# Fourteen picked groups instead of eleven, the first at group 3; the input check in pieces; the last edge tile as its own group

## The reference

```python
h = relu(layernorm(x))
x = x + sage3(h)          # three SAGE layers: mean over incoming edges @ Wl.T + b + h @ Wr.T, relu between
h = relu(layernorm(x))
messages = gelu((h[src] + edge_attr) @ We1 + be1) @ We2 + be2
aggregated = segment_sum(messages, dst)
x = x + gelu(((1 + eps) * h + aggregated) @ Wu1 + bu1) @ Wu2 + bu2
```

## Time and profile before

| | us |
|---|---|
| median of 3 executions | 976.62 |
| lowest, highest | 975.94, 2135.52 |
| profiled execution | 981.04 |
| its span in the trace | 979.3 |
| PE busy in it | 879.7 (90%) |
| PE weight loads | 653.8 (67%) |
| DVE busy | 485.6 (50%) |
| POOL busy | 383.6 (39%) |
| ACT busy | 250.2 (26%) |

### The profile page before, as it was taken

How to read it: one execution, slowest core, us unless ns; L and a number is a source line. 1 busy time by engine, 2 the same in 40 slices (tenths; PEclk the granted TensorE clock), 3 DMA queues, 4 the chain that set the end, 5 groups by cost and what they waited for, 6 DMA issues and landing times.

```text
span 979.3 us, 20510 instructions
## 1 busy us (share of the span) xinstructions
PE 879.7 (90%) x7824; PEld 653.8 (67%) x7824; DVE 485.6 (50%) x1882; ACT 250.2 (26%) x433; POOL 383.6 (39%) x411
## 2 busy tenths in 40 slices
PE   2977999999999999999809999999999899899883
PEld 1733555555554455555609999998988888898882
DVE  6589999995111121121348545445445545445431
ACT  2576677773110110011102111111111111111111
POOL 2000000000000001111277777777777777777771
PEclk9969999999999999999959999999999999999987
DMA  4200001102000000000174444444434444434321
GB/s 137 63 2 12 3 13 13 12 13 65 1 1 1 1 1 11 11 10 17 49 170 108 134 120 137 133 113 130 138 102 134 117 117 130 117 107 130 106 63 32
DMA packets 46635, 67.90 MB, mean 69 GB/s; under 512 B 15396, under 2 KB 25349, under 8 KB 46402
## 3 DMA queue, kind: packets, MB, share of 16 engines
q1 hardware_dynamic: 34626, 42.11, 15.5%
q0 software_dynamic: 11904, 24.40, 9.8%
HBM read 63.18 MB, written 3.30 MB: 68 GB/s over the span
## 4 chain that ended last, share of the span: by engine, by line
PE 64%; DVE 12%; POOL 10%; issue 7%; DMA 3%; ACT 2%; SPq 0%; ACTq 0%; POOLq 0%; DVEq 0%
PE f_ps L1132 26%; PE f_ps L1183 11%; POOL f_adj L545 10%; PE f_ps L1237 8%; PE f_ps L1168 7%; DVE f_region L594 2%; PE f_ps L1017 2%; DVE f_region L592 2%; PE f_ps L1010 2%; PE f_ps L1107 2%; DVE f_region L598 2%; DVE f_region L596 2%; DMA f_adj<-in_dst_next 1%; DMA inv<-f_rstd 1%; PE f_ps L1069 1%
## 5 line engine op out<-in xcount | busy, mean ns | idle before, releaser
L545 POOL DMA_INDIRECT f_adj<-table,f_table_idx x372 | 359.4, 966 | 113.4 <-issue 112.8
L1132 PE MATMUL f_ps<-f_adj,f_parts 125*128 125x500 fp8e4 (+1 forms) x1575 | 331.5, 352 | 0.1
L1132 PEld LDWEIGHTS f_ps<-f_adj,f_parts 125*128 125x128 bf16 x1575 | 143.5, 97 | 130.0 <-issue 11.1
L1183 PE MATMUL f_ps<-f_parts 125*128 125x128 bf16 x3300 | 200.0, 220 | 0.0
L1183 PEld LDWEIGHTS f_ps<-f_parts 125*128 125x128 bf16 x3300 | 193.2, 98 | 6.4 <-issue 4.4
L530 POOL TENSOR_TENSOR f_rest<-f_region,f_parts 125x512 f32<-125x512 f32 (+1 forms) x7 | 7.3, 1050 | 461.5 <-ACT f_parts L975 461.5
L1237 PE MATMUL f_ps<-f_adj 128*128 128x94 f32 (+20 forms) x984 | 131.9, 280 | 30.3 <-ACT f_adj L997 28.2
L870 DVE TENSOR_TENSOR f_adj<-f_ps,f_adj 128x512 f32<-128x512 f32 x93 | 64.1, 689 | 186.1 <-issue 116.0
L1237 PEld LDWEIGHTS f_ps<-f_adj 128*128 128x128 f32 x984 | 120.9, 195 | 37.9 <-issue 34.3
L997 ACT ACTIVATE f_adj<-f_adj 128x512 f32<-128x512 f32 x93 | 58.4, 630 | 336.8 <-DVE f_adj L870 332.5
L887 ACT CAST f_adj<-f_ps 128x500 f32 x213 | 126.1, 592 | 56.7 <-PE f_ps L1017 40.8
(11 more groups left out here) (135 smaller groups left out, 478.7 us busy)
## 6 DMA issues: line engine op xcount, KB each, us to landing
f_region<-in_edge_attr_T SPq DMA_DIRECT2D x104, 256.0 KB
f_adj<-table,f_table_idx POOLq DMA_INDIRECT x372
f_parts<-in_src_row SPq DMA_DIRECT2D x11, 256.0 KB, 3.7
f_adj<-inv SPq DMA_DIRECT2D x1, 1562.5 KB, 7.7
table<-f_region SPq DMA_DIRECT2D x6, 250.0 KB
out<-f_xT SPq DMA_DIRECT2D x6, 250.0 KB, 2.5
f_rcntT<-inv SPq DMA_DIRECT2D x5, 250.0 KB, 3.8
f_xT<-in_xT SPq DMA_DIRECT2D x1, 812.5 KB, 6.0
```

The costliest lines, as they stand in the source:

```text
L545: pool.indirect_dma_start(out=rows[:, r % RW, j * D:(j + 1) * D], out_offset=None, in_=table, in_offset=bass.IndirectOffsetOnAxis(ap=table ...
L1132: ins = pe.matmul(ps[:, dense_ps(i):dense_ps(i) + width(c)], parts[0:NP, (l % 2) * 3 + p, b, :], adj[0:NP, b, lo:hi].bitcast(F8), start=b ...
L1183: ins = pe.matmul(z_ps(g, j), select[0:NP, u % SELECT, j * P:(j + 1) * P], parts[0:NP, 3 + p, b, :], start=b == 0 and j == 0 and p == 0, s ...
```

## The change

It picks 14 groups instead of 11: 3, 10, 17, 24, 31, 39, 46, 53, 60, 68, 75, 82, 89, 97, so that the first has its 25 blocks in slots 0 to 2 (8, 8 and 9) and the others in the five to seven slots between two picked groups, three to five in each. Groups 0 to 102 have four tiles as before, group 103 has three, and tile 415 is group 104 (`FG` = 105); `tile(g)` gives a group's first tile, and the windows and bounds of the check follow. The check is split: `check_repeats` (the maximum over `c25`) goes into slot `CALM` = 221 of the dense stage, behind the slot's other DVE work; the rest goes into slots 0, 1, 2, 4, 8, 9 and 10 of the edge stage, behind the selections; PE's matmul of the flag moves from slot 0 to slot 12, and `keep_flag` from slot 2 to 13. The padding of the last tile's source numbers is 0, 1, 2, ... instead of zeros.

```diff
-        self.FG = -(-self.FT // self.FTG)
+        self.FG = -(-(self.FT - 1) // self.FTG) + 1
...
-        self.PERIOD = 9
-        self.picked = list(range(self.PERIOD - 1, self.FG - self.FTG, self.PERIOD))
+        self.SHARES = 14
+        reach = self.FG - 2 * self.FTG
+        self.picked = [self.FTG - 1 + i * (reach - self.FTG + 1) // (self.SHARES - 1) for i in range(self.SHARES)]
...
+    def tile(self, g):
+        return min(g * self.FTG, self.FT - 1) if g < self.FG else self.FT
+
     def tiles(self, g):
-        return min(self.FTG, self.FT - g * self.FTG)
+        return self.tile(g + 1) - self.tile(g)
...
+    CALM = GB + 8
...
+    FLAG, KEEP = 12, 13
...
+            def check_repeats():
+                dve.memset(flag[:, :], 0.0).then_inc(cleared, 1)
+                dve.wait_ge(cleared, 1)
+                dve.wait_ge(count_in[0], 16 * ((NC + 1) // 2))
+                dve.wait_ge(count_in[1], 16 * (NC // 2))
+                dve.tensor_reduce(flag[0:NB, 2:3], c25[0:NB, :], AX.X, ALU.max).then_inc(repeats, 1)
+                dve.wait_ge(repeats, 1)
+                dve.tensor_scalar(flag[0:NB, 2:3], flag[0:NB, 2:3], 15.5, None, ALU.is_gt).then_inc(repeats, 1)
...
                 for c in plan.due("rows_add", slot):
                     keep_rows(c)
+                if slot == CALM:
+                    check_repeats()
...
-            check_input()
             for g in range(END):
-                if g == 2:
+                if g == KEEP:
                     keep_flag()
...
                     for i, b in s.selections(g + 1):
                         select_sources(i, b)
-            dve.wait_ge(flagged, 11)
+                if g == 0:
+                    check_tiles()
+                if g == 1:
+                    check_steps()
+                if g == 2:
+                    check_windows()
+                if g == 4:
+                    join_checks()
+                if g == 8:
+                    check_order()
+                if g == 9:
+                    join_order()
+                if g == 10:
+                    join_all()
+            dve.wait_ge(flagged, 8)
...
-                    pe.wait_ge(flagged, 11)
+                    pe.wait_ge(flagged, 8)
...
-                if g == 0:
-                    pe.wait_ge(flagged, 9)
+                if g == FLAG:
+                    pe.wait_ge(flagged, 6)
                     pe.matmul(ps[0:1, 7 * BANK:7 * BANK + 1], flag[:, 3:4], unit[:, 0:1],
                               start=True, stop=True).then_inc(flagged, 1)
...
-    a["src_tiles"] = np.pad(src, (0, pad)).reshape(-1, P).T
+    a["src_tiles"] = np.concatenate([src, np.arange(pad, dtype=src.dtype)]).reshape(-1, P).T
```

More of the change, by code:

```diff
@@ L403, in edge_columns @@
         def edge_columns(g):
-            return t["edge_attr_T"][:, g * T * P:(g * T + s.tiles(g)) * P]
+            return t["edge_attr_T"][:, s.tile(g) * P:s.tile(g + 1) * P]
         def agg_ps(c, lo, hi):
@@ L751, in window_onehots @@
                     ins = dve.tensor_scalar(onehot[:, g % OH, j, 0:hi - lo], iota[:, 0:hi - lo], float(lo),
-                                            dst_abs[:, g * T + j:g * T + j + 1], ALU.add, ALU.is_equal)
+                                            dst_abs[:, s.tile(g) + j:s.tile(g) + j + 1], ALU.add, ALU.is_equal)
                 ins.then_inc(oh_ready, 1)
@@ L788, in node_add, with more, over, check_tiles @@
                                          op0=ALU.add, op1=ALU.add).then_inc(node_added, 1)
-            def check_input():
-                F, L = first[0:1, :], last[0:1, :]
-                F2, L2, FB, LB = F[:, 0:NT:2], L[:, 0:NT:2], F[:, 1:NT:2], L[:, 1:NT:2]
-                DG = s.DG
-                n_at = [0]
-                def more(count):
-                    n_at[0] += count
-                    return viol[0:1, n_at[0] - count:n_at[0]]
-                def over(a, gap, b):
-                    dve.scalar_tensor_tensor(out=more(a.shape[-1]), in0=a, scalar=float(gap), in1=b, op0=ALU.subtract,
-                                             op1=ALU.is_gt).then_inc(checked, 1)
+            F, L = first[0:1, :], last[0:1, :]
+            F2, L2, FB, LB = F[:, 0:NT:2], L[:, 0:NT:2], F[:, 1:NT:2], L[:, 1:NT:2]
+            DG = s.DG
+            n_at = [0]
+            def more(count):
+                n_at[0] += count
+                return viol[0:1, n_at[0] - count:n_at[0]]
+            def over(a, gap, b):
+                dve.scalar_tensor_tensor(out=more(a.shape[-1]), in0=a, scalar=float(gap), in1=b, op0=ALU.subtract,
+                                         op1=ALU.is_gt).then_inc(checked, 1)
+            small = [(0, 0.0, ALU.is_gt), (NT - 1, float(N - s.DW), ALU.is_lt)]
+            small += [(s.DT * (g + 1), float(e), ALU.is_lt) for e, g in zip(s.node_end, s.build_group) if g + 1 < GB]
+            def check_tiles():
                 over(L2, s.A_COLS // NB - 1, F2)
@@ L815, in check_input, with join_checks, check_order @@
                 dve.wait_ge(tile_in, 32)
-                over(bound[0:1, 0, :], 0.0, group_ends[0:1, 0, :])
+                over(bound[0:1, 0, :], s.MARGIN, group_ends[0:1, 0, :])
                 over(group_ends[0:1, 1, :], 0.0, bound[0:1, 1, :])
-                small = [(0, 0.0, ALU.is_gt), (NT - 1, float(N - s.DW), ALU.is_lt)]
-                small += [(s.DT * (g + 1), float(e), ALU.is_lt) for e, g in zip(s.node_end, s.build_group) if g + 1 < GB]
                 for i, limit, op in small:
                     dve.tensor_scalar(more(1), F[:, i:i + 1], limit, None, op).then_inc(checked, 1)
+            def join_checks():
                 dve.wait_ge(checked, 8 + len(small))
-                dve.memset(flag[:, :], 0.0).then_inc(flagged, 1)
-                dve.wait_ge(flagged, 3)
+                dve.wait_ge(cleared, 1)
                 dve.tensor_reduce(flag[0:1, 0:1], viol[0:1, 0:n_at[0]], AX.X, ALU.max).then_inc(flagged, 1)
+            def check_order():
                 dve.wait_ge(order_in, 32)
@@ L866, in _ @@
                         dve.wait_ge(z_ready, g + 1)
-                        dve.wait_ge(gathered[r % RW], 16 * (T * (r // RW) + s.tiles(g)))
+                        dve.wait_ge(gathered[r % RW], 16 * sum(s.tiles(s.of_ordinal(q)) for q in range(r % RW, r + 1, RW)))
                         if r >= PR:
@@ L1799, in layouts @@
     a["edge_attr_T"] = np.pad(ea.T, ((0, 0), (0, pad)))
-    a["src_tiles"] = np.pad(src, (0, pad)).reshape(-1, P).T
+    a["src_tiles"] = np.concatenate([src, np.arange(pad, dtype=src.dtype)]).reshape(-1, P).T
     a["src_row"] = np.pad(src, (0, pad))
     a["dst_tiles"] = np.pad(dst, (0, pad), constant_values=-1).reshape(-1, P).T
-    group = 4 * P
-    a["group_ends"] = np.concatenate([dst[0::group], dst[group - 1::group], dst[-1:]])[None]
+    starts = np.append(np.arange(0, dst.size - P, 4 * P), dst.size // P * P)
+    a["group_ends"] = dst[np.concatenate([starts, starts[1:] - 1, [dst.size - 1]])][None]
     for n in SAGE:
```

26 lines of the change are left out of this document (15 added, 11 removed).

## The result

The changed kernel takes 974.5 us in the median (971.59 to 976.08, 11 executions), the kernel before beside it 977.18: ratio 0.9964 [0.9952, 0.9977]. By the ratio 3.5 us are gained, by the two medians 2.7, where 8.6 were forecast. The profiled executions give 981.04 before and 975.46 after, -5.6. The bound moved as forecast, from POOL to PE, but POOL stands close behind it.

A forecast was written before the change was run, and what follows sets the result against it. POOL's 372 gathers bound the kernel; PE was to become the bound: 495.9 plus 459.7 gives 955.6, plus 3 handovers and 3.6 tail 962.2 against 971.2, so -9.0 us and a median of 968; 80% range 958 to 979.

The forecast's parts named there:

- the start of the selections: PE's first selection in the edge stage: 23.3 us won without the flag wait, 3.0 lost earlier, so 495.9.
- the stall of check_repeats: Dense stage, slot 221: the reduction delays agg(6), so PE stalls 3.0 us before mix(6); bounds 0 and 3.7.
- the sum of PE's steps: PE's edge-stage mixes, sums, selections, nodes and low clock: 459.7 us from 495.9, so the last sum ends at 955.6.
- PE-bound end: Main case: PE's stream sets the edge stage's end; 968 us, range 963 to 974, chance 0.66.
- handover idle: Rival: PE's 28.2 us of waits for messages in the edge stage stay; 993 us (976 to 1000), chance 0.13.
- low clock: Edge stage front: 1.5 us in PE's sum; as a rival about 19 us more over three slots, 985, chance 0.04.
- the added matmuls cost more than the old ones: Rival: the 900 added selection matmuls take 96 ns each instead of 56, 36 us more, 1004; chance 0.02.
- the handovers: Edge stage: PE's waits for gathered rows and other handovers add 3 us, bounds 0 and 10.
- the tail behind the last sum: End of the edge stage, last sum to end of node_add: 3.6 us instead of 4.7, with node_down(5) ahead.
- The median of the runs shown is 976.62, 4.4 below the profiled one, so 967.6: Last step: from the forecast profiled total of 972.0 to the median, said as 968.
- POOL needs 24 x 1.27: Edge stage gathers: 1.27 us per tile, 30.5 us per seven slots, against 32.0 for PE.
- POOL stays the bound: Rival: PE has more room and 360 gathers set the end, the last at 948.1; 961 us (957 to 963), chance 0.15.

The follow-up runs named there:

- e21: Changed kernel with check_repeats in slot 225 and 60 more matmuls in PE's wait before the first selection, on a chip without stalls: 968.05 us, 0.9907 of the kernel before.
- e9: The changed kernel again, unedited, on a chip with stalls: 1215.32 us, 1.0166 of the kernel before.
- e20: The changed kernel again, unedited, on a chip without stalls: 973.9 us, 0.9966 of the kernel before.
- e15: Kernel before with nearly all of PE's edge-stage matmuls left out, on a chip without stalls: 976.04 us, 0.9975 of the whole kernel before.
- e16: Changed kernel with nearly all of PE's edge-stage matmuls left out, on a chip without stalls: 968.91 us, 0.9905 of the whole kernel before.
- e18: e16 with a four-column memset in place of each DVE selection from the thirteenth on: 959.66 us, 0.9821 of the whole kernel before.
- e1: Changed kernel with check_repeats in slot 225 instead of 221, on a chip with stalls: 1205.69 us, 1.0094 of the kernel before.
- e10: e1's edit of the changed kernel again, on another chip with stalls: 1217.08 us, 1.0107 of the kernel before.
- e2: Changed kernel with the eleven picked groups of before, all else as changed, on a chip with stalls: 1218.38 us, 1.013 of the kernel before.
- e4: The kernel before, unedited, on another chip with stalls: 1203.59 us beside 1204.63.
- e12: Changed kernel with 11 of the 12 selection matmuls of each block left out, on a chip with stalls: 1087.21 us beside 1188.43 of the kernel before.
- e14: Kernel before with 11 of the 12 selection matmuls of each block left out, on a chip with stalls: 1090.63 us beside 1188.43 of the whole kernel.
- e3: Changed kernel with the rest of the check ahead of the slot loop and the flag in slot 0, chip with stalls: 1214.12 us, 1.0188 of the kernel before.

## Why the prediction was right or wrong

**Right.** PE as the new bound, the end of its wait for the flag, the start of the selections (495.9 forecast, 496.24 measured), the stall of check_repeats (3.0 forecast, 2.89 and a start of the edge stage 2.96 later), and the sum of PE's steps: 459.7 us forecast, 462.1 busy measured between 496.24 and the end of the last sum at 961.85. The windows all but without a gap and POOL's wait for the add of 0.6 us came as listed. The time, 974.5, lies in the 80% range of 958 to 979, and just outside the 963 to 974 given for a PE-bound end. The two slower rivals did not show: handover idle is 3.5 us, not 28, and eight blocks at the front cost 2.7 us of low clock, not 19. Nor did the added matmuls cost more than the old ones: eight blocks, 96 matmuls, take 5.52 us in e21, 57.5 ns each. (By the 81 ns of the Trainium skill's "TensorE: Matmul & The Clock Gate", "Back-to-back issue gap", they would be an estimated 7.8; the measurement decides.)

**Wrong: the gain.** 8.6 us were forecast, 2.7 (medians) or 3.5 (ratio) measured. Two steps failed, by about 3.5 us each.

The first is a row of small terms of PE's side. The selections start 0.3 later; PE's work is 2.4 more than summed, half of it the low clock at the front (8.06 us for eight blocks instead of 5.36, so 2.7 instead of 1.5), the other half not assigned; the handovers cost 3.5 instead of 3; the tail behind the last sum is 4.1 us instead of 3.6. Together 3.7: the chain ended 5.2 us earlier instead of 9.0. The low clock was mis-sized because it lasted longer than in the earlier trace rows, where it was 0.52 for the first 3 us of work and 1.00 from then on: here it was 0.50 from 496 to 500, 0.80 from 500 to 504 and 1.00 only behind that. The tail had it too (0.55 from 962 to 966); in e9, at 0.93, the tail took 3.2.

The second is the step "The median of the runs shown is 976.62, 4.4 below the profiled one, so 967.6". It took the distance of one execution from its median as a constant. For the changed kernel it was 1.0. Part of that distance is where PE's matmuls change from one rate to the other in the first 40 us. Timelines of PE of the changed kernel, first the profile after, then e20:

```profile
24.16 1.87 PE L1070 MATMUL f_ps<-f_xT,f_cent 128*128 128x500 f32 x2
25.83 1.68 PE L1073 MATMUL f_ps<-f_mean,f_xT 128*125 128x1 f32 x8
...
30.18 1.12 PE L1073 MATMUL f_ps<-f_mean,f_xT 128*125 128x1 f32 x8
```

```profile
23.86 1.00 PE L1070 MATMUL f_ps<-f_xT,f_cent 128*128 128x500 f32 x2
24.71 0.93 PE L1073 MATMUL f_ps<-f_mean,f_xT 128*125 128x1 f32 x8
```

The edge stage starts at 487.77 in the one and 484.37 in the other, and their times are 975.46 and 971.95: nearly all of the 3.5 us between two executions of one kernel is made there. The profiled execution of before changed late as well (L1028, the same matmuls, takes 1.87 us at 24.38 and 28.73), so the two profiles compare fairly, at -5.6.

But its 981.04 lies above every other execution of that kernel on such chips (975.94 to 980.48, the one very long aside). e15, whose dense stage is the same, shows why: it changed early, its edge stage starts at 481.75 instead of 484.81, and its gathers were a chain of 471.5 us instead of 472.5. So 3.1 of the profile's distance from its median come from the first 40 us and 1.0 from gathers. The eleven times of the changed kernel fall into two sets, 971.59 to 972.98 (five) and 974.50 to 976.08 (six); the late profile, 975.46, belongs to the second, and e20's early one, 971.95, would fit the first. So its median lies among the late ones, while that of before seems to lie among the early ones. That is read from the times, and not shown for executions without a profile.

So 3.4 us of the forecast gain (4.4 - 1.0) were a difference between one execution and its median.

**Wrong without effect.** "POOL needs 24 x 1.27", and with it 948.1 for the last gather's end: it was 955.62. A gather took 1.29 us from start to start, not 1.27. The forecast asked of the 19.8 us of selections only whether DVE had room, and not what they do to gathers. e15, e16 and e18 have 1.267, 1.275 and 1.256: selections cost gathers time, but in the kernels with little PE work the added ones, with the check's pieces, make only 0.008 of the 0.02; the rest shows up only with all of PE's work, and its cause stays open. (The Trainium skill's "GPSIMD Engine Reference", "8. Key points", says that GpSimd shares its SBUF interfaces with VectorE and contends with DVE instructions in a 2-port perf mode or with two SBUF inputs. e16 and e18, 971 against 953 ns a gather, show contention with DVE; in which mode its instructions ran no run shows, and the section has no price.)

Another sign that did not come: DVE's adds were to wait for PE's mixes. These waits fell from 64.8 to 12.9 us, those for gathers from 116.0 to 53.0, and DVE's longest total is now its one-hots' wait for PE's sums, 60.7.

Had PE been as free as in the rival "POOL stays the bound", its 961 would have been 968.9 (e16). From the last gather's end to the chain's end there are 10.3 us (profile after) and 11.5 (e20), where e16, which only gathers bound, needs 8.9: the gathers are no more than 1.4 to 2.6 us behind PE, and less work on PE would soon meet them.

**Not foreseen.** The wait of PE in slot 221 can cost its length again by the clock (seen on one chip with stalls), and on chips where PE's stream stalls by itself the change is slower: by 1.66% (e9). How often such chips are met the runs don't say.

**A better version.** check_repeats in slot 225 keeps all of the change and gives 969.05 us on a chip without stalls, 0.9909 [0.9895, 0.9924] of the kernel before. On chips with stalls it is still slower than the kernel before (e1 1.0094, e10 1.0107).

## What to carry to other kernels

When work moves from one engine to another, price it three times: on the engine that gets it, on the one that loses it, and on the third that prepares it, whose operations can make the first one's slower though it has room itself. A long operation that nobody waits for must not be put right ahead of one that somebody does; look for the next slot with slack, here four further on. And take differences between executions in the same condition: see first where the two profiles lie within their runs, and don't carry the distance of one from its median into the forecast of the other.

## What the runs showed that was not expected

- PE's stream in the edge stage stalls on some chips by itself, mostly by 0.3 to 2.6 us at a time and once by 3.7 (e2), before (e4) and after the change (e9), and also with most matmuls of the selections left out (e12 to e14, there up to 7.6). The dense stage of e4 and e9 has no such waits. The cause stays open.
- The rate of PE's matmuls near 24 us differs between executions of one kernel (1.87 against 1.00 us for the same two) while the granted clock of the windows reads 1.00 in both; it changes at about 24 (e20), 30 (the profile after) or 36 us (e21).

```profile
28.00:32.00 4.00, 4.00 (x22) 2.90 (x21) 1.62 (x8) 1.74 (x3) 0.00 (x0) 1.00 0.37 97
```

```profile
28.00:32.00 4.00, 4.00 (x34) 3.38 (x35) 1.62 (x8) 1.87 (x4) 0.00 (x0) 1.00 0.35 91
```

  These are windows of the changed kernel, in the profile after and in e20: 22 matmuls and 34 in the same 4 us.
- An indirect gather of 128 rows takes mostly 0.94 us of POOL, and up to 2.44 beside DVE operations that follow each other without a pause (above).
- A granted clock of 0.16 to 0.18 from 1000 us on, for hundreds of microseconds (e3).
